# A first part of queries and keys from PSUM, a stack of which five rows in eight are written, and score maxima with two heads a tile

## The reference, cut to what matters

```python
def _L0_xattn_ref(query, key, value, Wq, bq, Wk, bk, Wv, bv, Wo, bo):
    q = (query @ Wq + bq).reshape(Bq, Sq, H, DK)
    k = (key @ Wk + bk).reshape(Bq, Sk, H, DK)
    v = (value @ Wv + bv).reshape(Bq, Sk, H, DK)
    scores = jnp.einsum('bqhd,bkhd->hbqk', q, k) / np.sqrt(DK)
    attn = jax.nn.softmax(scores.reshape(H * Bq, Sq, Sk), axis=0).reshape(H, Bq, Sq, Sk)
    return jnp.einsum('hbqk,bkhd->bqhd', attn, v).reshape(Bq, Sq, H * DK) @ Wo + bo

x = x + jnp.tanh(g_xattn[0]) * _L0_xattn_ref(_layernorm(x), ctx_1024, ctx_1024, Wq, bq, Wk, bk, Wv, bv, Wo, bo)
x = x + jnp.tanh(g_ffn[0]) * _L0_ffn_ref(_layernorm(x), clip_x, clip_down, w_gate, w_up, w_down)
```

## Time and profile before

| | us |
|---|---|
| runs of the kernel before | 994.38, 995.92, 996.14 (median 995.92) |
| the profiled execution, its own time | 996.3 |
| its span, first to last instruction | 994.4 |
| PE, DVE, ACT, POOL busy in the span | 793.8, 869.2, 674.1, 442.5 |
| mean granted TensorE clock | 0.940 |

### The profile page before, as it was taken

One profiled execution on the slowest core, in us unless ns is written; L12 is line 12 of the kernel. 1 busy time (PEld: TensorE's weight loads), 2 busy tenths in 40 slices (PEclk: granted clock), 3 DMA queues, 4 the chain that ended last, 5 costly groups with the idle time before them and its releaser, 6 DMA issues. The chain is left out here.

```text
span 994.4 us, 21125 instructions
## 1 busy us (share of the span) xinstructions
PE 793.8 (80%) x8184; PEld 443.8 (45%) x8184; DVE 869.2 (87%) x1044; ACT 674.1 (68%) x981; POOL 442.5 (44%) x330
## 2 busy tenths in 40 slices
PE   3798891777777768999999998999989886177666
PEld 1465550111111135666566665666556565022233
DVE  6679851999999969999999998999989969778868
ACT  3254571999999967777767776777767413576683
POOL 4133240000000005888878888788868855122300
PEclk9799895999999979999999999999999899598979
DMA  9489798444555836587566955687665742000013
GB/s 290 172 260 359 257 332 315 167 171 169 194 204 193 296 112 175 160 241 249 148 195 189 310 161 165 165 268 225 162 170 161 223 151 100 1 0 1 0 44 127
DMA packets 112393, 180.92 MB, mean 182 GB/s; under 512 B 10032, under 2 KB 37296, under 8 KB 112304
## 3 DMA queue, kind: packets, MB, share of 16 engines
q1 hardware_dynamic: 112304, 179.67, 57.4%
HBM read 137.70 MB, written 41.94 MB: 181 GB/s over the span
## 5 line engine op out<-in xcount | busy, mean ns | idle before, releaser
L795 POOL TENSOR_TENSOR e<-e,recip 128x640 f32<-128x640 f32 (+3 forms) x256 | 348.1, 1403 | 101.4 <-DVE recip L837 101.4
L770 ACT ACTIVATE e<-ps_att 128x512 f32<-128x512 f32 x512 | 308.7, 666 | 116.1 <-PE ps_att L705 116.0
L826 DVE TENSOR_REDUCE pair_sums<-e 128x128 f32<-128x2048 f32 x128 | 292.1, 2282 | 19.5 <-ACT e L770 18.8
L701 PE MATMUL ps_att<-shift,minus 128*128 128x512 bf16 x512 | 199.1, 389 | 18.4 <-DMA arena<-k_stack 6.6
L705 PE MATMUL ps_att<-arena 128*128 128x128 bf16 x2048 | 200.1, 221 | 0.0
L553 ACT ACTIVATE copies<-ps_max 128x1024 bf16<-128x1024 f32 x192 | 179.1, 1028 | 20.8 <-PE ps_max L533 20.6
L723 PE MATMUL acc<-e,arena 128*32 128x128 f32 x4096 | 179.6, 295 | 10.9 <-DVE e L807 10.4
L533 PE MATMUL ps_max<-q_head,k_head 128*128 128x512 bf16 x512 | 138.6, 387 | 60.5 <-DVE high L572 21.7
L705 PEld LDWEIGHTS ps_att<-arena 128*128 128x128 bf16 x2048 | 159.1, 99 | 62.0 <-issue 2.7
L723 PEld LDWEIGHTS acc<-e,arena 128*32 128x32 f32 x4096 | 107.1, 111 | 40.4 <-issue 13.4
L807 DVE TENSOR_TENSOR e<-e,recip_v 128x384 f32<-128x384 f32 (+3 forms) x256 | 118.0, 505 | 0.0
(11 more groups left out here) (127 smaller groups left out, 822.1 us busy)
## 6 DMA issues: line engine op xcount, KB each, us to landing
arena<-k_stack SPq DMA_DIRECT2D x256, 256.0 KB, 2.8
k_stack<-parts SPq DMA_DIRECT2D x64, 256.0 KB, 3.8
q_stack<-parts SPq DMA_DIRECT2D x64, 256.0 KB, 3.7
k_head<-k_stack SPq DMA_DIRECT2D x16, 1024.0 KB, 5.6
q_head<-q_stack SPq DMA_DIRECT2D x16, 1024.0 KB, 7.8
arena<-q_stack SPq DMA_DIRECT2D x64, 256.0 KB, 4.8
arena<-in_x_dram SPq DMA_DIRECT2D x5, 1024.0 KB, 8.1
arena<-in_ctx_dram SPq DMA_DIRECT2D x4, 1024.0 KB, 6.4
```

The costliest lines, as they stand in the source:

```text
L701: nc.tensor.matmul(ps[half][:], minus[:], shift_at(qc, kc).to_broadcast([P, HB, P]), start=True, stop=False, skip_group_check=True)
L770: nc.scalar.activation(e_at(qc * STEPS + i, half * HB, (half + 1) * HB).rearrange("p q b i -> p b q i"), ps[half][:].rearrange("p (b q i) ...
L795: nc.gpsimd.tensor_tensor(part, part, by_pairs(recip[:, kc % 2, :], share), ALU.mult).then_inc(pool_scaled, 1)
L826: nc.vector.tensor_reduce(pair_sums[:, :, h // 2, :], e[:, g % RING // 2].rearrange("p q s b i -> p q i (s b)"), AX.X, ALU.add).then_inc(s ...
```

## The change

**In prepare**, ACT writes part 1 straight from PSUM, with the bias; the copy in `full` is gone, and DVE makes the rest from PSUM, bias and part 1 in one instruction. There are five PSUM slots, and PE now waits for DVE's `rest` to free one. V's projection, bias and store are gone from this stage, and POOL's large fill with zeros is replaced by two fills of the gaps only, one at the end of the stage and one at the start of the next. ctx and the K weights are loaded first, and ACT waits for each weight alone. From the second block on the groups go K, Q, K, Q. The rows of a stack are ordered so that 64 rows hold the four largest products; SP writes five of eight rows, and the others are copied inside DRAM during `maxima`, in five DMAs of 2 or 4 MB. SP no longer waits for the last writes in this stage; it issues the loads of the first two pairs of heads there.

**In maxima**, the scores come from the first 64 rows of each stack alone. Two heads lie in the 128 partitions, and a tile is made by two matmuls on the two halves of the array's rows. There are 64 groups again, of one pair of heads and one batch. Only two PSUM slots of 1024 are left for tiles that ACT copies, one is for DVE's, and two banks hold V: after the group's last tile, in every fourth group, PE projects V for two batches, with a one-row float32 matmul for the bias and four of 256 columns, and ACT stores it after the copies of the next group. The constants for `attend` are set here by POOL.

**In ffn**, POOL multiplies for j = 1, 3, 5 where it did for 2 and 4, and DVE makes the integers after j = 0.

```diff
-K_PARTS = (0, 0, 1, 1, 0, 2, 1, 2)
-Q_PARTS = (0, 1, 0, 1, 2, 0, 2, 1)
+K_PARTS = (0, 0, 1, 1, 2, 2, 0, 1)
+Q_PARTS = (0, 1, 0, 1, 0, 1, 2, 2)
+K_WRITTEN = (0, 1, 2, 3, 4)
+Q_WRITTEN = (0, 1, 2, 3, 6)
+WRITES = len(K_WRITTEN)
+K_COPIED = ((5, 4, 1), (6, 0, 1), (7, 2, 1))
+Q_COPIED = ((4, 0, 2), (7, 6, 1))
...
+V_LEN = (H // 2) * 3 * DK
+GB = 3
...
+def load_pair(sp, hp, k_stack, q_stack, k_head, q_head, loaded):
+    for j in range(LANES):
+        rows = slice(j * HALF, (j + 1) * HALF)
+        for head, stack in ((k_head, k_stack), (q_head, q_stack)):
+            sp.dma_start(head[rows, hp % 2], stack[:, hp * LANES + j, 0:HALF, :].rearrange("c p x -> p c x")
+                         ).then_inc(loaded[hp % 2], 16)
...
+            return (g // DC, g % DC) if c == 0 else (g % 2, g // 2)
...
+                load_ctx(0)
+                sp.dma_start(wk_s, wk.rearrange("(c p) n -> p c n", p=P)).then_inc(s["wk_loaded"], 16)
+                load_x(0)
+                sp.dma_start(wq_s, wq.rearrange("(c p) n -> p c n", p=P)).then_inc(s["wq_loaded"], 16)
...
+                        for r in written:
                             sp.dma_start(stack[c, h0:h0 + H // DC, r * DK:(r + 1) * DK, :].rearrange("h d x -> d h x"),
-                                         parts[:, u % GB, part, :]).then_inc(stacked[u % GB], 16)
-                for i in range(GB):
-                    sp.wait_ge(stacked[i], 16 * 8 * len(range(i, NC * 2 * DC, GB)))
+                                         parts[:, u % GB, plan[r], :]).then_inc(stacked[u % GB], 16)
+                        if u == NC * GROUPS - 2:
+                            for i, count in written_before(u):
+                                sp.wait_ge(stacked[i], count)
+                            load_pair(sp, 0, k_stack, q_stack, keep["k_head"], keep["q_head"], keep["head_loaded"])
+                load_pair(sp, 1, k_stack, q_stack, keep["k_head"], keep["q_head"], keep["head_loaded"])
...
-                pool.memset(vpad[:], 0.0).then_inc(s["v_zeroed"], 1)
...
+                pool.wait_ge(s["part3_ready"], NC * UN)
+                pool.wait_ge(s["w_turned"], 3 * IC)
+                pool.memset(spare[:, 0:LATE * V_LEN].rearrange("p (r e d) -> p r e d", e=3, d=DK)[:, :, 1, :], 0.0
+                            ).then_inc(keep["v_zeroed"], 1)
...
-                    if u >= 4:
-                        pe.wait_ge(s["full_ready"], u - 3)
+                    if u >= PSLOTS:
+                        pe.wait_ge(s["rest_ready"], u - PSLOTS + 1)
...
-                        if i % 2:
-                            project_v(c, i // 2)
...
-                        nc.scalar.activation(full[:, u % UB, :], psP[:, u % 4, :], ACT.Identity,
-                                             bias=bias[:, dc:dc + 1]).then_inc(s["full_ready"], 1)
+                        if g >= GB and n == 0:
+                            act.wait_ge(stacked[g % GB], 16 * WRITES * (g // GB))
+                        nc.scalar.activation(parts[:, g % GB, 0, n * BANK:(n + 1) * BANK], psP[:, u % PSLOTS, :],
+                                             ACT.Identity, bias=bias[:, dc:dc + 1]).then_inc(s["part1_ready"], 1)
...
-                                             ACT.Copy).then_inc(s["part1_ready"], 1)
...
-                        nc.vector.tensor_tensor(rest[:, u % UB, :], full[:, u % UB, :],
-                                                parts[:, g % GB, 0, n * BANK:(n + 1) * BANK],
-                                                ALU.subtract).then_inc(s["rest_ready"], 1)
+                        nc.vector.scalar_tensor_tensor(
+                            out=rest[:, u % UB, :], in0=psP[:, u % PSLOTS, :], scalar=(bk_s, bq_s)[m][:, dc:dc + 1],
+                            in1=parts[:, g % GB, 0, n * BANK:(n + 1) * BANK], op0=ALU.add, op1=ALU.subtract
+                        ).then_inc(s["rest_ready"], 1)
...
+        ps_copy = es.enter_context(nc.psum_tensor("ps_copy", [P, 2, LANES * S], F32))
+        ps_direct = es.enter_context(nc.psum_tensor("ps_direct", [P, LANES * S], F32))
+        psV = es.enter_context(nc.psum_tensor("psV", [P, 2, BANK], F32))
...
+                def copy_rows(stack, dst, src, n):
+                    sp.dma_start(stack[:, :, dst * DK:(dst + n) * DK, :].rearrange("c h d x -> (c h) (d x)"),
+                                 stack[:, :, src * DK:(src + n) * DK, :].rearrange("c h d x -> (c h) (d x)")
+                                 ).then_inc(rows_copied, 16)
+                for i in range(GB):
+                    sp.wait_ge(stacked[i], 16 * WRITES * len(range(i, NC * 2 * DC, GB)))
+                later = [(k_stack, *rows) for rows in K_COPIED] + [(q_stack, *rows) for rows in Q_COPIED]
+                copy_rows(*later[0])
+                for hp in range(2, PAIRS):
+                    sp.wait_ge(to_max, (hp - 1) * B)
+                    load_pair(sp, hp, k_stack, q_stack, k_head, q_head, loaded)
+                    if hp - 1 < len(later):
+                        copy_rows(*later[hp - 1])
...
+                def tile(dst, hp, b, kc):
+                    for j in range(LANES):
+                        rows = slice(j * HALF, (j + 1) * HALF)
+                        last = nc.tensor.matmul(
+                            dst[:, j * S:(j + 1) * S], k_head[rows, hp % 2, kc, b * P:(b + 1) * P],
+                            q_head[rows, hp % 2].rearrange("p c (b q) -> p c b q", q=P)[:, :, b, :], start=True, stop=True)
+                    return last
+                def project_v(v):
+                    c, b2 = v // (B // 2), v % (B // 2)
+                    if v == 0:
+                        pe.wait_ge(keep["v_weights_loaded"], 32)
+                    if v >= 2:
+                        pe.wait_ge(v_stored, v - 1)
+                    nc.tensor.matmul(psV[:, v % 2, :], ones[0:1, :], bv_s[0:1, :].rearrange("p (a n) -> p a n", a=1)
+                                     .to_broadcast([1, 2, D]), start=True, stop=False, skip_group_check=True)
+                    for j in range(2):
+                        b = 2 * b2 + j
+                        for kc in range(DC):
+                            last = nc.tensor.matmul(psV[:, v % 2, j * D:(j + 1) * D], cT[:, c, kc, b * P:(b + 1) * P],
+                                                    wv_s[:, kc, :], start=False, stop=kc == DC - 1, skip_group_check=True)
+                    last.then_inc(v_projected, 1)
+                for g in range(GROUPS):
+                    hp, b = g // B, g % B
+                    if b == 0:
+                        pe.wait_ge(loaded[hp % 2], (hp // 2 + 1) * 16 * 2 * LANES)
+                    for kc in range(COPIED):
+                        a = g * COPIED + kc
+                        if a >= 2:
+                            pe.wait_ge(copied, a - 1)
+                        tile(ps_copy[:, a % 2, :], hp, b, kc).then_inc(to_copy, 1)
+                    if g:
+                        pe.wait_ge(updated, 2 * g - 1)
+                    tile(ps_direct, hp, b, COPIED).then_inc(to_max, 1)
+                    if v_unit(g) is not None:
+                        project_v(v_unit(g))
...
+                for g in range(GROUPS):
+                    if g >= RING:
+                        act.wait_ge(updated, 2 * (g - RING) + 2)
+                    for kc in range(COPIED):
+                        a = g * COPIED + kc
+                        act.wait_ge(to_copy, a + 1)
+                        nc.scalar.activation(copies[:, g % RING, kc, :], ps_copy[:, a % 2, :], ACT.Copy).then_inc(copied, 1)
+                    if g >= 1 and v_unit(g - 1) is not None:
+                        store_v(v_unit(g - 1))
...
-        POOL_J = (2, 4)
+        POOL_J = (1, 3, 5)
...
-                            if j == 4 and n + 2 < NB:
+                            if j == 0 and n + 2 < NB:
```

284 lines of the change are left out of this document (119 added, 165 removed).

## The result

| | before | after |
|---|---|---|
| runs, us | 994.38, 995.92, 996.14 | 1043.15, 1045.59, 1052.5, 1056.77 |
| median, us | 995.92 (995.71 beside the runs of after) | 1049.05 |
| ratio, 95% interval | | 1.0531 [1.0477, 1.0585] |
| the profiled execution's own time; its span | 996.3; 994.4 | 1056.77; 1055.0 |
| mean granted TensorE clock | 0.940 | 0.841 |

The forecast was 986.2 in a range of 970 to 1014.

The account below looks back on a forecast made before the run. The prediction took DMA to bound prepare and the tied ACT and DVE to bound maxima. From 996.3 us: prepare -44.5, maxima +43.0, attend -0.6, ffn -8.0, giving 986.2, range 970 to 1014.

Parts of the forecast that it names:

- The read of the bound: In maxima ACT and DVE are tied without a gap; whatever is put on ACT or makes it wait adds time.
- Prepare, first block: Start and first block of prepare: 15.0 us saved, so the second block starts at 46.1.
- Second, third and fourth block: In prepare: second block 23.9 us and third 26.8, together 10.1 saved; fourth block 4.5 saved.
- From the last part to `maxima`: End of prepare: 6.6 us from last part to PE's first maxima tile in place of 19.6, 13.0 saved.
- its three terms: After the last part: five writes 3.8 us, issue of the second pair's loads 2.0, end of the block 0.9.
- Stores of V: In maxima, 16 stores on ACT at 0.59 us each add 9.4 us.
- PE's V before the next tile: In maxima, ACT waits 2.1 us for PE at each of 16 V: 33.6 us longer, bounds 27 to 51.
- The fall: Rival: TensorE's clock falls in maxima, 2.59 us more per V; 1007 us if half fall, 1027 if all; chance 0.25.
- Attend and ffn: Attend starts 0.6 us sooner; ffn's gate and up period falls from 8.95 to 7.4 to 7.9, saving 8 us.
- Halves one after the other: Rival in maxima: a tile's two halves do not run side by side, stalls 2.6 to 3.2, 994 to 1004 us; chance 0.15.
- DMA-bound `prepare`: Rival: prepare stays bound by DMA, writes queue behind loads, saving 36 us there, 995 us in all; chance 0.13.

Follow-up runs that it names:

- e2: The changed kernel plus an unused bf16 matmul of 512 columns for each of four tiles in the 48 groups without V: 997.55 us, ratio 1.0038 to before.
- V in pieces: The changed kernel with each V projection in maxima split into six pieces over four groups, each behind one tile: 962.35 us, ratio 0.9658 to before.

## Why the prediction was wrong, step by step

**The read of the bound was right.** ACT and DVE are tied in `maxima`, what makes ACT wait is added to the time, and ACT's waits lie where they were placed: 16 of them, before the first copy behind each V, and nowhere else.

**Prepare, first block.** The second block starts at 48.57, predicted 46.1. PE's wait ends at 34.7 instead of 33.6 and the first units run at the low clock. Missed by 2.5.

**Second, third and fourth block.** 24.8 and 26.7 us against 23.9 and 26.8, and the fourth begins at 100.1 and has its last part at 121.1, 21.0 against 21.2. These steps held, and with them the reading that PE and DVE take over when SP no longer lags.

**From the last part to `maxima`**: 14.2 us where I counted 6.6 (its three terms add up to 6.7). This is the mis-sized term of `prepare`. Two chains end together there, and both were too short. SP: the first pair's loads stand ahead of the last group's writes (2.9 us, not counted), the second pair's take 5.6 to issue where I had 2.0, and the block's end 1.6 where I had 0.9. The landing: I let the first pair's loads "land meanwhile"; they are issued only once the last part is ready (121.45 against 121.1) and need until 135, since loads of 64 partitions move half as much per us as those of 128: 13.8 us from issue to use, and 13.0 in the run where these loads stood alone. Moving the second pair's loads shows that the landing alone is enough to hold PE.

**Stores of V**: 0.48 us each from start to start, 7.7 in all, against 0.59 and 9.4.

**PE's V before the next tile**: 2.1 us x 16 = 33.6 predicted; 2.23 x 16 = 35.7 at the full clock (e2), 5.5 x 16 = 87.7 in after. The mechanism and its size at the full clock were right. This is the step that failed: the term was priced at the full clock, and all 16 V ran at the low one. The fall stood among the rivals. I gave the fall a chance of 0.25, with "each V is itself dense work" against it. The timeline shows the clock rising just behind each V, too late for it, and gone before the next. The share of PE in the records can't decide it: it was 139 of 184 us before, at 0.98, and is as high in after, 211 of 278, at 0.60; V in pieces has it too, at 1.00. The rule of the Trainium skill that the prediction cited for this rival (TensorE: Matmul & The Clock Gate, Part 1) speaks of an idle array; here the clock fell over an engine that the records show three quarters busy, and in the earlier trace rows, which the prediction called in agreement, PE was busy for 1.27 of 3 us. That the low clock costs this time, and that the order of the same matmuls can hold it up, is shown; why the clock falls in one order and not in the other stays open.

**The rival's price was too small as well.** It had 2.59 us more for each V, 1027 in all. The stall grew by 3.4 (5.61 - 2.23): V by 2.7 (5.7 against 2.98), and the rest is with the tiles on either side of it, which the rival had as hidden. With 16 x 3.4 = 54 on the forecast, plus the 10.6 missed in `prepare`, it is 1051, and the median is 1049. That these lie so close is in part luck: the profiled execution, at 1056.8, is the forecast plus 50.6 in `maxima`, 10.6 in `prepare`, 8.9 in the residual stage and 0.6 elsewhere.

**Attend and ffn.** -0.7 against -0.6. The period is 8.05 against 7.4 to 7.9, so from first to last `sil` 8.5 us are saved; the all-reduce comes 5.97 us after POOL's last product, before as after, and with j = 5 that product is later: 1.7 lost between the last maximum and the next rounding where I had 1.

**The residual stage** was in no term. The 8.9 us are a collision that the change only shifted in time; without it the profiled execution would be near 1048, close to the median.

**The other rivals.** Halves one after the other: two matmuls of a tile take 0.61 us together at the low clock and 0.39 at the full one, where one after the other they took 0.61 at the full clock; it falls. DMA-bound `prepare`: it falls for the blocks (their lengths came out as worked out from PE and DVE; the DMA share is 0.93 in the second and 0.57 in the third), and holds in the transition alone, where DMA is full from 118 to 135.

## What to carry to other kernels

When work on TensorE is made cheaper, the clock can fall for the work beside it (0.98 to 0.60 here), even where the records show the engine as busy as before: before dense float32 work is put among light tiles, price it at both clocks, and spread it in pieces that the buffers can bridge rather than in one lump. Half the partitions in a load is half its rate, so a transfer that gets smaller by leaving rows out is not faster by that. And where an engine is "hidden", ask behind which buffer: with two slots it is hidden for one copy, not for a V.

## What the runs showed of the hardware

- Adding 192 unused matmuls to PE made the kernel 5% faster (1049 to 998), by the granted clock alone (0.60 to 0.98 in `maxima`).
- Two bf16 matmuls of 64 rows and 512 columns on the two halves of the array take 0.39 us together at the full clock and 0.61 at the low one. A float32 bias row (one row, 512 columns, two instructions in the trace) takes 2.07 us at the low clock, over half of the 3.78 of V's four float32 matmuls of 128 rows and 256 columns (eight instructions).
- A change of the array's partition costs 0.1 to 0.2 us at the full clock: two inside V account for 0.39 of its 2.98.
- Loads of 64 partitions move 206 to 213 GB/s with the DMA engines full, loads of 128 387 to 400, also at 256 KB each.
- A DVE instruction of 128x8 elements in SBUF takes 0.17 us alone and up to 2.28 beside POOL's adds of 2.33 each; it then ends with one of them. Not every one does: the reciprocal of the same size took 0.20 beside the same adds. The Trainium skill (SBUF — State Buffer, Who interferes with whom) calls the port pair that the two share an exclusive lock; this trace agrees, as did the 9.55 us beside the fill of 10.34 in the earlier trace rows.
- POOL's all-reduce across partitions begins 5.7 to 6.7 us after POOL's instruction before it where it ends the gate and up blocks, in each of the profiles, with nothing to wait for.
